# Two-layer graph attention on one core: float8 masks, an OR check of the kept masks, a reordered layer change and a last run closed in two halves

## The chip, the cores and the metric

The kernel runs on one core of one Trainium2 chip. The metric is the device time of one execution in microseconds, as the median of several runs. TensorE is called PE in the rows, VectorE DVE, ScalarE ACT, GpSimd POOL, SyncE SP.

## The reference

There are N = 4096 nodes with 128 features, an adjacency matrix adj of N x N int32 (0 or 1, some 0.2% ones, symmetric, ones on the diagonal), and two attention layers. Each is followed by a residual sum and a layer norm.

```python
# layer 0: H = 4 heads of D = 32
Wh = (h @ W).reshape(N, H, D)
e = s_src[:, None, :] + s_dst[None, :, :]          # per head, s = Wh . a
e = jnp.where(e >= 0, e, 0.2 * e)
e = jnp.where(adj[:, :, None] > 0, e, NEG_INF)
attention = jax.nn.softmax(e, axis=1)
h0 = jax.nn.elu(jnp.einsum('ijh,jhd->ihd', attention, Wh).reshape(N, H * D))
x = _layernorm(x + h0)
# layer 1: one head of 128
x_tan = _logmap0(x)
e = jax.nn.leaky_relu(x_tan @ a[:D] + (x_tan @ a[D:]).T, 0.2)
attention = jax.nn.softmax(jnp.where(adj > 0, e, NEG_INF), axis=1)
x = _layernorm(x + _proj(_expmap0(attention @ x_tan)))
```

## The kernel before

The attention is never formed. exp(leaky(s_i + d_j)) is a product of a factor of i and one of j on either side of the sign of s_i + d_j. So the kernel makes two 0/1 masks from the adjacency, the neighbours above and those below, and TensorE multiplies both with weighted features, split into three bf16 parts. The masks are float8, four to an int32.

**Masks.** GpSimd's queue loads the adjacency with a cast from int32 to one byte (adj_tiles). TensorE transposes the bytes in pairs, seen as bf16, and ScalarE copies them from the bank to masks, scaled so that a 1 becomes 0xC0 and a 0 becomes 0x80 (L451, L471). SyncE stores each of the four column blocks of masks (masks_kept, 4 MB each) for the second layer.

**First layer.** Four column blocks (NC) of 32 units each: ScalarE or VectorE makes the signs, VectorE the masks, TensorE the 64 matmuls (L613). take_head takes a head out of the banks, close_piece closes a block of rows (ELU, norm, the two dots for the second layer) in five pieces.

**Second layer.** 32 row tiles in NR = 8 runs of RT = 4 tiles. A run has 256 matmuls, two banks per tile, so all eight banks belong to one run. Its stationary operands are the masks, its moving ones the weighed features, in four groups (NG = 4) of 8 tiles. A group is made by weigh_group (VectorE, two sides), round_part1 (ScalarE cast), take_high1 (VectorE difference), round_part1 again and take_middle1. In runs 0 and 1 TensorE goes group by group (L972), from run 2 on tile by tile (L985). Groups 0 to 2 need nothing of the first layer's last block; group 3 needs all of close_piece, roots, logs and gains for it.

For a run e, SyncE loads its kept masks (load_masks, 2 MB) and scores (load_s1) when run e - 2 is done, ScalarE makes signs for half of the columns (signs, L695), VectorE compares the rest and splits the masks (split_group, L710 to L722). The banks are emptied by evacuate_run (L730), tile by tile, and finish_run closes the run: it asks ScalarE for a square root, a tanh and a square root (Closing.dve and Closing.act, L339). The order on VectorE after the first runs is: evacuate_run(e), finish_run(e), split_group(e + 2). TensorE begins tile t of run e + 1 when pair t of run e is out of the banks (pair_taken).

**Checks.** The masks hold only if adj has nothing but 0 and 1. 128 loads of 512 KB each bring all of adj once more, unchanged, to five buffers; ScalarE takes the square of 2a - 1 with a sum (check_part, L750), in batches after signs in runs 0 to 6. raise_flag (VectorE, after finish_run of run 6) waits for them all, joins them with the ranges of scores, and sends a flag that a general version would be chosen by; it then ends in nothing for these inputs.

All waits are written out as semaphores; each engine goes through its instructions in the order in which the code lists them.

Of the kernel before, what the change touches and what calls it, by code (L numbers as in the profile page):

```python
# [19 lines left out]
BOTH_SIGNS = float(0x8080)  # L20

# [40 lines left out]
def two_layer_gat(nc, x, adj, W, a0, a1, out):  # L62
# [8 lines left out]
    adj_flat = adj.rearrange("(p k) n -> p (k n)", p=P)  # L71
# [53 lines left out]
    CHECKS = 128  # L125
    CHECK = N * N // P // CHECKS
# [9 lines left out]
    with ctx:  # L136
# [19 lines left out]
        minus_one = sb("minus_one", [P, 1], F32, fast)  # L156
# [3 lines left out]
        checks = sb("checks", [P, CHECKS], F32, fast)  # L160
# [8 lines left out]
        adj_tiles = sb("adj_tiles", [P, AHEAD, N], U8, fast)  # L169
# [41 lines left out]
        def of_ring(*shape):  # L211
# [8 lines left out]
        late_sides = [of_ring(GT, K1).rearrange("p (t k) -> p t k", k=K1) for _ in range(2)]  # L220
# [11 lines left out]
            mean_var=of_ring(RT, 2).rearrange("p (t k) -> p t k", k=2))  # L232
        free = (NG - 1) * GT * W1
# [3 lines left out]
        check_out = [s_rows[:, 1, :].bitcast(FP8)[:, n * CHECK:(n + 1) * CHECK] for n in range(4)]  # L237
# [6 lines left out]
        def j_tile1(half, j):  # L244
# [28 lines left out]
        minus_ready, check_done, odd_ready, odd_in, flag_ready = sems(  # L273
            "minus_ready", "check_done", "odd_ready", "odd_in", "flag_ready")
# [5 lines left out]
        class Closing:  # L280


            def __init__(self, name, work, result, small, stats, mean_var, inv_std):
                self.work, self.result, self.small, self.stats, self.mean_var = work, result, small, stats, mean_var
                self.inv_std = inv_std
                self.asked, self.given, self.ready = sems(f"{name}_asked", f"{name}_given", f"{name}_ready")
                self.stored = sems(f"{name}_stored0", f"{name}_stored1")

            def dve(self, step, v, e):
                dve, y = step.engine, e % 2  # L290
                raw2, raw, scratch, norm, gain, big, root = (self.small[:, k, :] for k in range(7))
                work, result = self.work, self.result[:, y, :, :]
# [3 lines left out]
                dve.wait_ge(self.given, e * 3 + 1)  # L296
# [5 lines left out]
                inv = self.inv_std[:, e * RT:(e + 1) * RT]  # L302
                last = dve.tensor_tensor(result, feat[:, e * RT:(e + 1) * RT, :], over(inv, RT, F), ALU.mult)
                result_at = step.post(last)
                dve.wait_ge(self.given, e * 3 + 2)
# [10 lines left out]
                step(dve.tensor_tensor(work, v, over(gain, RT, F), ALU.mult))  # L316
                step.need(result_at)
                step(dve.tensor_tensor(result, result, work, ALU.add))
                for t in range(RT):
                    last = dve.bn_stats(self.stats[:, t, 0:6], result[:, t, :])  # L320
                step(last)
                for t in range(RT):
                    last = dve.bn_aggr(self.mean_var[:, t, :], self.stats[:, t, 0:6])
                step(last)
                dve.tensor_scalar(raw2, self.mean_var[:, :, 1], LN_EPS, None, ALU.add).then_inc(self.asked, 1)
                dve.wait_ge(self.given, e * 3 + 3)
                newton_root(step, root, raw2, scratch)
                step(dve.reciprocal(root, root))
                for t in range(RT):
                    last = dve.tensor_scalar(result[:, t, :], result[:, t, :], self.mean_var[:, t, 0:1], root[:, t:t + 1],  # L330
# [3 lines left out]
            def act(self, act, e):  # L334
                raw2, raw, scratch, norm, gain, big, root = (self.small[:, k, :] for k in range(7))
                for n, (to, frm, func) in enumerate(((raw, norm, ACT.Sqrt), (gain, scratch, ACT.Tanh),
                                                     (root, raw2, ACT.Sqrt))):
                    act.wait_ge(self.asked, e * 3 + (n + 1))
                    act.activation(to, frm, func).then_inc(self.given, 1)  # L339

            def store(self, sp, e):
                sp.wait_ge(self.ready, e + 1)
                sp.dma_start(out_rows[:, e * (RT // 2):(e + 1) * (RT // 2), :], paired(self.result[:, e % 2, :, :]))\
                    .then_inc(self.stored[e % 2], 16)

            def all_stored(self, sp):
                for y in range(2):
                    sp.wait_ge(self.stored[y], 16 * (NR // 2))
# [97 lines left out]
        def take_quarter(act, k, some=range(CT // 2)):  # L446
            for m in some:
# [5 lines left out]
                               ACT.Copy, bias=BOTH_SIGNS, scale=float(TWO)).then_inc(turned_out, 1)  # L453
# [13 lines left out]
        def take_group(act, c, q):  # L467
# [5 lines left out]
                           ACT.Copy, bias=BOTH_SIGNS, scale=float(TWO)).then_inc(turned_out, 1)  # L473
# [175 lines left out]

        def weigh_group(dve, g):  # L650
            sides = early_sides if g == 0 else late_sides
            js = slice(g * GT, (g + 1) * GT)
            for b in range(2):
                if g > 1:
                    dve.wait_ge(moving1_ready, 2 * g)
# [7 lines left out]
        def take_high1(dve, g):  # L663
            sides = early_sides if g == 0 else late_sides
            for b in range(2):
                dve.wait_ge(cast1_given, 4 * g + b + 1)
                dve.tensor_tensor(sides[b], sides[b], moving_part(g, b, 0), ALU.subtract).then_inc(cast1_asked, 1)

        def take_middle1(dve, g):
            sides = early_sides if g == 0 else late_sides  # L670
            for b in range(2):
                dve.wait_ge(cast1_given, 4 * g + 2 + b + 1)
# [3 lines left out]
        def round_part1(act, g, q):  # L676
            sides = early_sides if g == 0 else late_sides
            for b in range(2):
                act.wait_ge(cast1_asked, 4 * g + 2 * q + b + 1)
# [45 lines left out]
        def evacuate_run(dve, e):  # L725
            for t in range(RT):
# [723 lines left out]
```

## Time and profile before

| | before |
|---|---|
| median of 3 runs | 979.15 us (977.76 to 983.52) |
| the profiled execution's own time | 978.17 us |
| its span | 976.3 us |
| TensorE busy | 854.6 us (88%) |
| VectorE busy | 771.7 us (79%) |
| ScalarE busy | 759.4 us (78%) |
| first layer's matmuls end | about 558.4 us |
| last matmul ends | about 937.6 us |

A row of a timeline gives the start in us from the span's start, the duration, engine, line, operation, what is written and read, how many instructions were merged, and in brackets how long the engine idled before and what ended that. The page's groups give busy us and mean ns.

### The profile page before, as it was taken

What the parts mean: (1) busy time and instruction counts of PE and PEld (TensorE: products, weight loads), DVE (VectorE), ACT (ScalarE), POOL (GpSimd) and SP (SyncE); (2) the same over time, 40 slices, a digit from 0 to 9 for tenths busy, and PEclk for the clock granted to TensorE, in tenths of its full rate; (3) what the DMA queues carried; (4) which work ended last, traced back from release to release, by engine and by line L of the source; (5) the groups of instructions that cost most, each with busy time, mean ns of one, the idle gap of its engine ahead of it and who ended that gap; (6) DMA issues with size and microseconds to landing.
All of it is one profiled execution on the core that took longest, in us unless ns stands there. A gap on an engine that the chain in (4) does not pass through costs nothing.

```text
span 976.3 us, 24788 instructions
## 1 busy us (share of the span) xinstructions
PE 854.6 (88%) x10868; PEld 698.6 (72%) x10868; DVE 771.7 (79%) x1415; ACT 759.4 (78%) x933; POOL 94.9 (10%) x177
## 2 busy tenths in 40 slices
PE   8468999989999899999999992999999999899940
PEld 6468999989999899999998951555555555455520
DVE  3857898899988999889977897986859594949316
ACT  3868988888999879999889865367877686868751
POOL 2200000000000000000000100003131222212210
PEclk9879999999999999999999997899999999999975
DMA  8988278704568045040300040209494949576750
GB/s 143 172 83 203 64 71 95 222 24 49 66 75 228 24 39 73 25 196 23 110 3 24 19 177 1 98 12 361 170 388 152 402 152 368 190 308 220 279 211 12
DMA packets 55731, 135.01 MB, mean 138 GB/s; under 512 B 7746, under 2 KB 32708, under 8 KB 54980
## 3 DMA queue, kind: packets, MB, share of 16 engines
q0 software_dynamic: 26240, 83.90, 36.8%
q1 hardware_dynamic: 29380, 49.50, 13.9%
q8 instruction: 86, 1.41, 0.6%
q14 instruction: 25, 0.20, 0.1%
HBM read 162.60 MB, written 21.12 MB: 188 GB/s over the span
## 4 chain that ended last, share of the span: by engine, by line
PE 42%; DVE 26%; DMA 13%; ACT 11%; issue 7%; SPq 0%; DVEq 0%; ACTq 0%
PE bank L613 32%; DMA ring<-in_adj_dram 5%; PE bank L985 4%; ACT masks L695 4%; DMA moving<-in_adj_dram 4%; DVE ring L561 4%; DMA s_rows<-score_rows 3%; DVE ring L580 3%; ACT ring L548 2%; PE bank L464 2%; ACT s_rows L750 2%; ACT masks L451 2%; DVE ring L590 1%; PE bank L972 1%; DVE ring L584 1%
## 5 line engine op out<-in xcount | busy, mean ns | idle before, releaser
L613 PE MATMUL bank<-moving,ring 128*128 128x99 bf16 (+1 forms) x6400 | 461.8, 220 | 10.7 <-DVE ring L590 7.6
L613 PEld LDWEIGHTS bank<-moving,ring 128*128 128x128 fp8e4 x6400 | 390.9, 98 | 15.2 <-DVE ring L590 8.6
L548 ACT ACTIVATE ring<-s_rows,scores 128x1024 fp8e4<-128x1024 f32 x356 | 377.5, 1142 | 15.6 <-PE bank L613 14.2
L613 PE MATMUL bank<-moving,masks 128*128 128x99 bf16 x1792 | 243.3, 210 | 26.5 <-DVE ring L580 15.6
L613 PEld LDWEIGHTS bank<-moving,masks 128*128 128x128 fp8e4 x1792 | 176.7, 99 | 28.3 <-DVE ring L580 16.5
L985 PE MATMUL bank<-moving,masks 128*128 128x387 bf16 x1152 | 195.6, 328 | 0.0
L985 PEld LDWEIGHTS bank<-moving,masks 128*128 128x128 fp8e4 x1152 | 112.7, 98 | 79.1
L580 DVE SCALAR_TENSOR_TENSOR ring<-ring,masks 128x1024 int32<-128x1024 int32 x89 | 108.3, 1217 | 4.7 <-ACT ring L548 4.6
L590 DVE TENSOR_TENSOR ring<-masks,ring 128x1024 int32<-128x1024 int32 x72 | 88.2, 1225 | 26.4 <-PE bank L613 24.6
L750 ACT ACTIVATE s_rows<-moving,minus_one 128x1024 fp8e4<-128x1024 int32 x76 | 86.9, 1144 | 26.9 <-DMA moving<-in_adj_dram 26.3
L561 DVE TENSOR_SCALAR ring<-s_rows,neg_d 128x1024 uint8<-128x1024 f32 x156 | 106.9, 750 | 0.0
L695 ACT ACTIVATE masks<-s_rows,adj_tiles 128x512 fp8e4<-128x512 f32 x144 | 89.3, 709 | 1.1 <-DMA s_rows<-score_rows 0.9
L972 PE MATMUL bank<-moving,masks 128*128 128x387 bf16 x384 | 66.7, 335 | 20.6 <-DVE masks L722 20.6
L985 PE MATMUL bank<-adj_tiles,masks 128*128 128x387 bf16 x384 | 69.3, 333 | 11.9 <-DVE ring L730 11.9
L972 PEld LDWEIGHTS bank<-moving,masks 128*128 128x128 fp8e4 x384 | 38.0, 100 | 49.1 <-DVE masks L722 21.8
L750 ACT ACTIVATE s_rows<-ring,minus_one 128x1024 fp8e4<-128x1024 int32 x52 | 59.4, 1143 | 12.5 <-DMA ring<-in_adj_dram 12.2
L985 PEld LDWEIGHTS bank<-adj_tiles,masks 128*128 128x128 fp8e4 x384 | 37.6, 99 | 40.6 <-DVE ring L730 13.9
L471 ACT ACTIVATE masks<-bank 128x1024 uint16<-128x1024 uint16 x48 | 48.5, 1016 | 19.6 <-PE bank L464 18.6
L896 POOL DMA_DIRECT2D ring<-in_adj_dram x52 | 27.7, 533 | 357.2 <-PEq L621 180.8
L50 DVE TENSOR_SCALAR ring<-ring 128x4 f32<-128x4 f32 x16 | 2.7, 170 | 70.1 <-ACT ring L339 70.1
L896 POOL DMA_DIRECT2D moving<-in_adj_dram x76 | 40.8, 538 | 134.1 <-ACT s_rows L750 130.8
L584 DVE TENSOR_TENSOR ring<-ring,masks 128x1024 int32<-128x1024 int32 x39 | 47.5, 1218 | 0.0
(183 smaller groups left out, 750.6 us busy)
## 6 DMA issues: line engine op xcount, KB each, us to landing
moving<-in_adj_dram POOLq DMA_DIRECT2D x76, 512.0 KB, 6.6
ring<-in_adj_dram POOLq DMA_DIRECT2D x52, 512.0 KB, 6.3
masks_kept<-masks SPq DMA_DIRECT2D x4, 4096.0 KB, 18.4
masks<-masks_kept SPq DMA_DIRECT2D x8, 2048.0 KB, 23.7
adj_tiles<-in_adj_dram POOLq DMA_DIRECT2D x24, 512.0 KB, 8.4
s_rows<-score_rows SPq DMA_DIRECT2D x14, 512.0 KB, 5.7
adj_tiles<-in_adj_dram POOLq DMA_DIRECT2D x16, 256.0 KB, 15.1
feat<-in_x_dram SPq DMA_DIRECT2D x4, 512.0 KB, 5.7
```

The costliest lines, as they stand in the source:

```text
L471: act.activation(dst[:, j:j + GQ, t * P:(t + 1) * P], turn_bank[q % 4][:, :].bitcast(U16).rearrange("p (j i) -> p j i", i=P), ACT.Copy, bi ...
L548: last = act.activation(j_tile(below, k), s_rows[:, h % 2, :], ACT.Sign, bias=scores[:, g * JU + k, h:h + 1], saturate=False)
L561: last = dve.tensor_scalar(j_tile(below, k), s_rows[:, h % 2, :], neg_d[:, h, j:j + 1], float(TWO), ALU.is_lt, ALU.mult)
L580: dve.scalar_tensor_tensor(out=below, in0=below, scalar=1, in1=m, op0=ALU.logical_shift_right, op1=ALU.bitwise_and).then_inc(done, 1)
L584: dve.tensor_tensor(below, below, m, ALU.bitwise_and).then_inc(done, 1)
L590: dve.tensor_tensor(above_slot(c, u).bitcast(I32), m, below, ALU.bitwise_xor).then_inc(unit_ready, 1)
L613: last = pe.matmul(bank[b][:, at + lo:at + hi], mask, moving[:, j, h, lo:hi], start=first, stop=(j == T - 1), skip_group_check=True)
L695: last = act.activation(j_tile1(sides_of_run[y][1], j), s_rows1[:, y, :], ACT.Sign, bias=d1[:, j:j + 1], saturate=False)
L750: act.activation(check_out[k % 4], check_in[k % CB], ACT.Square, bias=minus_one[:, 0:1], scale=2.0, accum_out=checks[:, k:k + 1], saturate ...
L896: pool.dma_start(check_in[k % CB], adj_flat[:, k * CHECK:(k + 1) * CHECK]).then_inc(check_loaded[k % CB], 16)
L972: last = pe.matmul(bank[2 * t + side][:, 0:PARTS * K1], j_tile1(sides_of_run[e][side], j)[:, t * P:(t + 1) * P], moving1(g)[:, j % GT, sid ...
L985: last = pe.matmul(bank[2 * t + side][:, 0:PARTS * K1], j_tile1(sides_of_run[e % 2][side], j)[:, t * P:(t + 1) * P], moving1(j // GT)[:, j ...
```

## The change

1. The adjacency is cast to float8 instead of uint8 on its load. A 1 is then 0x38, and ScalarE's copies scale by 8/7 instead of 64 (0x38 x 8/7 = 0x40). Any value but 0 and 1 leaves other bits.
2. The check reads the kept masks (16 MB) and not the adjacency (64 MB): 32 loads of 512 KB, to two buffers instead of five, and 32 ORs on VectorE into one tile (seen), instead of 128 squares on ScalarE. raise_flag folds the tile to 64 words, takes the six low bits of each byte and their maximum.
3. The second layer's groups 1 to 3 have two pairs of buffers for the weighed sides. Groups 1 and 2 are weighed one behind the other, pieces of close_piece come in between, and ScalarE's order changes too.
4. The last run is emptied, closed and stored in two halves of two tiles; evacuate_run, finish_run and Closing get bounds lo and hi.

```diff
-    CHECKS = 128
-    CHECK = N * N // P // CHECKS
+    CHECKS = 32
+    CHECK = N * N // P // 4 // CHECKS
...
-        adj_tiles = sb("adj_tiles", [P, AHEAD, N], U8, fast)
+        adj_tiles = sb("adj_tiles", [P, AHEAD, N], FP8, fast)
...
-        late_sides = [of_ring(GT, K1).rearrange("p (t k) -> p t k", k=K1) for _ in range(2)]
+        late_sides = [[of_ring(GT, K1).rearrange("p (t k) -> p t k", k=K1) for _ in range(2)] for _ in range(2)]
...
-        check_in = [of_ring(CHECK).bitcast(I32) for _ in range(2)] + \
-            [moving_flat[:, free + n * 2 * CHECK:free + (n + 1) * 2 * CHECK].bitcast(I32) for n in range(3)]
+        seen, *check_in = [moving_flat[:, free + n * 2 * CHECK:free + (n + 1) * 2 * CHECK].bitcast(I32) for n in range(3)]
         CB = len(check_in)
...
-                               ACT.Copy, bias=BOTH_SIGNS, scale=float(TWO)).then_inc(turned_out, 1)
+                               ACT.Copy, bias=BOTH_SIGNS, scale=ONE_TO_TWO).then_inc(turned_out, 1)
...
-        def check_part(act, k):
-
-            act.wait_ge(check_loaded[k % CB], 16 * (k // CB + 1))
-            if k >= 4:
-                act.wait_ge(check_done, k - 3)
-            act.activation(check_out[k % 4], check_in[k % CB], ACT.Square, bias=minus_one[:, 0:1], scale=2.0,
-                           accum_out=checks[:, k:k + 1], saturate=False).then_inc(check_done, 1)
+        def check_part(dve, k):
+
+            dve.wait_ge(check_loaded[k % CB], 16 * (k // CB + 1))
+            dve.wait_ge(check_done, k + 1)
+            dve.tensor_tensor(seen, seen, check_in[k % CB], ALU.bitwise_or).then_inc(check_done, 1)
+
+        def begin_checks(dve):
+            dve.memset(seen, 0)
+            dve.memset(low_bits.bitcast(U8), 0x3F).then_inc(check_done, 1)
...
+            n = CHECK
+            while n > CHECK // 16:
+                n //= 2
+                step(dve.tensor_tensor(seen[:, 0:n], seen[:, 0:n], seen[:, n:2 * n], ALU.bitwise_or))
+            step(dve.tensor_tensor(seen[:, 0:n], seen[:, 0:n], low_bits, ALU.bitwise_and))
...
                 for k in range(CHECKS):
                     if k >= CB:
-                        pool.wait_ge(check_done, k - CB + 1)
-                    pool.dma_start(check_in[k % CB], adj_flat[:, k * CHECK:(k + 1) * CHECK]).then_inc(check_loaded[k % CB], 16)
+                        pool.wait_ge(check_done, k - CB + 2)
+                    if k == 0:
+                        pool.wait_ge(kept, 16 * NC)
+                    pool.dma_start(check_in[k % CB], kept_flat[k // (CHECKS // NC), :, (k % (CHECKS // NC)) * CHECK:
+                                                               (k % (CHECKS // NC) + 1) * CHECK]).then_inc(check_loaded[k % CB], 16)
...
@@ ScalarE, layer change @@
                 act.wait_ge(moving1_ready, 2)
+                elu_exp(act, NC - 1)
+                round_part1(act, 1, 0)
+                round_part1(act, 2, 0)
+                round_part1(act, 1, 1)
                 signs(act, 0, 1)
-                round_part1(act, 1, 0)
-                round_part1(act, 1, 1)
-                elu_exp(act, NC - 1)
+                round_part1(act, 2, 1)
                 signs(act, 0, 2)
-                round_part1(act, 2, 0)
-                round_part1(act, 2, 1)
...
@@ ScalarE, the runs @@
-                for e in range(NR):
-                    fast_closing.act(act, e)
+                for e in range(NR - 1):
+                    fast_closing.act(act)
                     if e + 2 < NR:
                         for g in range(NG):
                             signs(act, e + 2, g)
-                    while done < min(CHECKS, CHECKS * (e + 1) // (NR - 1)):
-                        check_part(act, done)
-                        done += 1
+                fast_closing.act(act, 0, RT // 2)
+                fast_closing.act(act, RT // 2, RT)
...
@@ VectorE, layer change @@
                 weigh_group(dve, 1)
+                weigh_group(dve, 2)
                 take_high1(dve, 1)
+                close_piece(NC - 1, 0)
                 take_middle1(dve, 1)
                 split_group(dve, 0, 1)
-                close_piece(NC - 1, 0)
-                weigh_group(dve, 2)
                 take_high1(dve, 2)
+                close_piece(NC - 1, 1)
                 take_middle1(dve, 2)
                 split_group(dve, 0, 2)
-                for n in range(1, 5):
+                for n in range(2, 5):
                     close_piece(NC - 1, n)
...
@@ VectorE, the runs @@
-                for e in range(NR):
+                done = 0
+                for e in range(NR - 1):
                     evacuate_run(dve, e)
...
                     if e + 2 < NR:
                         for g in range(NG):
                             split_group(dve, e + 2, g)
+                    if e == 0:
+                        begin_checks(dve)
+                    while done < CHECKS * max(e - 1, 0) // (NR - 3) and done < CHECKS:
+                        check_part(dve, done)
+                        done += 1
                     if e == NR - 2:
                         raise_flag(step)
+                for lo in (0, RT // 2):
+                    evacuate_run(dve, NR - 1, lo, lo + RT // 2)
+                    finish_run(step, NR - 1, lo, lo + RT // 2)
```

The change moves instructions at three places. The first is the layer change on ScalarE. Before, from the first set of signs of run 0 (L695) to the first casts of the second layer (L680) and ELU's exp (L646):

```order
L695 ACTIVATE masks<-s_rows,adj_tiles 128x512 x16
L680 ACTIVATE moving<-ring 128x8x129 x4
L646 ACTIVATE second_part<-first_part 128x1024
L695 ACTIVATE masks<-s_rows,adj_tiles 128x512 x8
L680 ACTIVATE moving<-ring 128x8x129 x4
```

Of the change, where these lines are L700, L685 and L648:

```order
L700 ACTIVATE masks<-s_rows,adj_tiles 128x512 x8
L648 ACTIVATE second_part<-first_part 128x1024
L685 ACTIVATE moving<-ring 128x8x129 x6
L700 ACTIVATE masks<-s_rows,adj_tiles 128x512 x8
L685 ACTIVATE moving<-ring 128x8x129 x2
L700 ACTIVATE masks<-s_rows,adj_tiles 128x512 x8
```

Of the sixteen signs, eight now stand behind the exp and six casts. The same place on VectorE, of the change, from the weighing of groups 1 and 2 (L661) over the differences (L672, L678), the ELU sums (L396, L398) and the norm's first piece (L403) to the splits (L720, L727):

```order
L672 TENSOR_TENSOR ring<-ring,moving 128x1032 x2
L396 SCALAR_TENSOR_TENSOR second_part<-second_part,feat 128x1024
L398 SCALAR_TENSOR_TENSOR second_part<-first_part,second_part 128x1024
L678 TENSOR_TENSOR moving<-ring,moving 128x8x129 x2
L720 SCALAR_TENSOR_TENSOR masks<-masks 128x1024
L727 TENSOR_TENSOR masks<-masks 128x1024
L672 TENSOR_TENSOR ring<-ring,moving 128x1032 x2
L403 BN_STATS stats<-second_part 128x6 x8
L678 TENSOR_TENSOR moving<-ring,moving 128x8x129 x2
```

Pieces of the closing now stand between the two differences of a group; before they stood behind the splits. The second place is VectorE between two runs: of the change, the end of the splits for run 4, the first batch of ORs (L756, the buffers are parts of moving), and run 3's sums out of the banks (L735):

```order
L715 TENSOR_SCALAR masks<-s_rows,adj_tiles 128x512 x4
L720 SCALAR_TENSOR_TENSOR masks<-masks 128x512
L725 TENSOR_TENSOR masks<-masks 128x512
L727 TENSOR_TENSOR masks<-masks 128x1024
L756 TENSOR_TENSOR moving<-moving 128x1024 x6
L735 TENSOR_REDUCE ring<-bank 128x129 x8
```

The six ORs are new there; before, the sums followed the splits. The third is VectorE after the closing of run 6, where raise_flag follows the last batch and the last run's sums come in two halves:

```order
L756 TENSOR_TENSOR moving<-moving 128x1024 x7
L798 TENSOR_TENSOR moving<-moving 128x512
L798 TENSOR_TENSOR moving<-moving 128x256
L798 TENSOR_TENSOR moving<-moving 128x128
L798 TENSOR_TENSOR moving<-moving 128x64
L799 TENSOR_TENSOR moving<-moving,ring 128x64
L801 TENSOR_REDUCE odd<-scores 128x1
```

The seven ORs and five folding steps are new ahead of the flag's own instructions.

## Rows read from the trace of the kernel before

**Rows 1.** The page: the span.
```profile
span 976.3 us, 24788 instructions
```
**Rows 2.** Timeline, TensorE: group 3, starts of runs 2 to 4, last stretch.
```profile
612.13 12.92 PE L972 MATMUL bank<-moving,masks 128*128 128x387 bf16 x64 [19.10 <-DVE masks L722]
...
667.50 2.83 PE L985 MATMUL bank<-adj_tiles,masks 128*128 128x387 bf16 x16
...
712.04 2.84 PE L985 MATMUL bank<-adj_tiles,masks 128*128 128x387 bf16 x16 [1.76 <-DVE ring L730]
...
757.05 2.84 PE L985 MATMUL bank<-adj_tiles,masks 128*128 128x387 bf16 x16 [2.23 <-DVE ring L730]
...
929.47 8.15 PE L985 MATMUL bank<-moving,masks 128*128 128x387 bf16 x48
```
**Rows 3.** Timeline, VectorE, three starts of L730; then the page's group of the wait.
```profile
665.93 3.82 DVE L730 TENSOR_REDUCE ring<-bank 128x129 f32<-128x387 f32 x8
...
710.96 3.82 DVE L730 TENSOR_REDUCE ring<-bank 128x129 f32<-128x387 f32 x8
...
730.39 0.17 DVE L50 TENSOR_SCALAR ring<-ring 128x4 f32<-128x4 f32 x1 [11.02 <-ACT ring L339]
...
755.97 3.82 DVE L730 TENSOR_REDUCE ring<-bank 128x129 f32<-128x387 f32 x8
...
L50 DVE TENSOR_SCALAR ring<-ring 128x4 f32<-128x4 f32 x16 | 2.7, 170 | 70.1 <-ACT ring L339 70.1
```
**Rows 4.** Timeline, VectorE, from the last wait to the end.
```profile
944.78 0.42 DVE L785 TENSOR_REDUCE odd<-scores 128x1 f32<-128x256 f32 x1 [24.79 <-ACT s_rows L750]
...
950.69 3.83 DVE L730 TENSOR_REDUCE ring<-bank 128x129 f32<-128x387 f32 x8
954.55 1.23 DVE L739 TENSOR_TENSOR ring<-ring,adj_tiles 128x1032 f32<-128x1032 f32 x1
...
963.29 0.69 DVE L316 TENSOR_TENSOR ring<-ring 128x512 f32<-128x512 f32 x1
...
964.74 0.87 DVE L320 BATCH_NORM_STATS2 ring<-ring 128x6 f32<-128x128 f32 x4
...
967.73 1.12 DVE L330 TENSOR_SCALAR ring<-ring 128x128 f32<-128x128 f32 x4
```
**Rows 5.** The page: a VectorE operation on two operands of 1024 int32.
```profile
L590 DVE TENSOR_TENSOR ring<-masks,ring 128x1024 int32<-128x1024 int32 x72 | 88.2, 1225 | 26.4 <-PE bank L613 24.6
```
**Rows 6.** DMA: issues at 658.61 and 659.74, all 128, a chain step, stores.
```profile
ring<-in_adj_dram POOLq DMA_DIRECT2D x1, 512.0 KB, 3.9
...
ring<-in_adj_dram POOLq DMA_DIRECT2D x1, 512.0 KB, 4.5
...
DMA to landing us min/median/max: 3.8/6.6/9.7
...
660.59 0.28 issue
...
out_dram<-ring SPq DMA_DIRECT2D x8, 256.0 KB, 2.2
```
**Rows 7.** Busy by stretch (us, PE, PEld, DVE, ACT, POOL, PEclk, DMA, GB/s); timeline, layer change.
```profile
560.00:580.00 20.00, 19.63 (x119) 11.35 (x118) 19.90 (x23) 15.69 (x18) 1.41 (x3) 1.00 0.63 236
...
560.55 1.22 DVE L656 TENSOR_TENSOR ring<-feat,adj_tiles 128x1024 f32<-128x1024 f32 x1
...
547.53 9.92 ACT L695 ACTIVATE masks<-s_rows,adj_tiles 128x512 fp8e4<-128x512 f32 x16
561.89 4.65 ACT L680 ACTIVATE moving<-ring 128x1032 bf16<-128x1032 f32 x4 [4.44 <-DVE ring L657]
...
567.38 5.00 ACT L695 ACTIVATE masks<-s_rows,adj_tiles 128x512 fp8e4<-128x512 f32 x8
```
**Rows 8.** DMA issues with a cast; busy by stretch, the first 50 us.
```profile
adj_tiles<-in_adj_dram POOLq DMA_DIRECT2D x24, 512.0 KB, 8.4
...
0.00:50.00 50.00, 31.54 (x245) 27.64 (x246) 29.80 (x64) 30.13 (x38) 12.70 (x25) 0.90 0.99 156
```

More of the change, by code:

```diff
@@ L287, in __init__, with dve @@
                 self.stored = sems(f"{name}_stored0", f"{name}_stored1")
[L289 to L292, printed above, removed]
+                self.turns, self.answers, self.stores = 0, 0, [0, 0]
+            def dve(self, step, v, e, lo=0, hi=RT):
+                dve, y, tiles = step.engine, e % 2, hi - lo
+                raw2, raw, scratch, norm, gain, big, root = (self.small[:, k, lo:hi] for k in range(7))
+                work, result = self.work[:, lo:hi, :], self.result[:, y, lo:hi, :]
+                before = self.turns
+                self.turns += 3
                 step(dve.tensor_tensor(work, v, v, ALU.mult))
@@ L315, in dve @@
                 step(dve.tensor_tensor(gain, gain, scratch, ALU.mult))
-                step(dve.tensor_tensor(work, v, over(gain, RT, F), ALU.mult))
+                step(dve.tensor_tensor(work, v, over(gain, tiles, F), ALU.mult))
                 step.need(result_at)
                 step(dve.tensor_tensor(result, result, work, ALU.add))
-                for t in range(RT):
-                    last = dve.bn_stats(self.stats[:, t, 0:6], result[:, t, :])
+                for t in range(tiles):
+                    last = dve.bn_stats(self.stats[:, lo + t, 0:6], result[:, t, :])
@@ L321, in dve @@
                 step(last)
-                for t in range(RT):
-                    last = dve.bn_aggr(self.mean_var[:, t, :], self.stats[:, t, 0:6])
+                for t in range(tiles):
+                    last = dve.bn_aggr(self.mean_var[:, lo + t, :], self.stats[:, lo + t, 0:6])
                 step(last)
-                dve.tensor_scalar(raw2, self.mean_var[:, :, 1], LN_EPS, None, ALU.add).then_inc(self.asked, 1)
-                dve.wait_ge(self.given, e * 3 + 3)
+                dve.tensor_scalar(raw2, self.mean_var[:, lo:hi, 1], LN_EPS, None, ALU.add).then_inc(self.asked, 1)
@@ L327, in dve @@
+                dve.wait_ge(self.given, before + 3)
                 newton_root(step, root, raw2, scratch)
                 step(dve.reciprocal(root, root))
-                for t in range(RT):
-                    last = dve.tensor_scalar(result[:, t, :], result[:, t, :], self.mean_var[:, t, 0:1], root[:, t:t + 1],
+                for t in range(tiles):
+                    last = dve.tensor_scalar(result[:, t, :], result[:, t, :], self.mean_var[:, lo + t, 0:1], root[:, t:t + 1],
                                              ALU.subtract, ALU.mult)
@@ L332, in dve, with act @@
                 last.then_inc(self.ready, 1)
[L334 to L338, printed above, removed]
+            def act(self, act, lo=0, hi=RT):
+                raw2, raw, scratch, norm, gain, big, root = (self.small[:, k, lo:hi] for k in range(7))
+                for to, frm, func in ((raw, norm, ACT.Sqrt), (gain, scratch, ACT.Tanh), (root, raw2, ACT.Sqrt)):
+                    self.answers += 1
+                    act.wait_ge(self.asked, self.answers)
```

86 lines of the change are left out of this document (43 added, 43 removed).

## The prediction

> **What bounds the kernel now.** I read the page first, then TensorE's timeline through the second layer, then VectorE's, then the DMA issues. The span is 976.3 us [rows 1], of which TensorE is busy for the greatest part. In the second layer its runs of 256 matmuls follow each other: run 2 starts at 667.50, run 3 at 712.04 after 1.76 us of waiting, run 4 at 757.05 after 2.23. A run thus takes 712.04 - 1.76 - 667.50 = 42.8 us [rows 2]. The waits, 11.9 us in five places, are all for VectorE's sums out of the banks (L730). The last matmul ends near 937.6.
>
> VectorE's loop explains them [rows 3]. From one L730 to the next (710.96 to 755.97) it takes 45.0 us, of which it idles 11.0 at L50: it has asked ScalarE for a square root (L339), and ScalarE first finishes its batch of adjacency checks (L750). Over six runs these idles are 10.96, 11.02, 10.76, 13.11, 11.88 and 8.31, together 66.0 of the page's 70.1 us. Without the idle (some 0.27 is left of it where ScalarE is free: the group's ten others share 4.1 us) the loop is 45.0 - 10.75 = 34.3 us: 3.9 of L730, 14.3 of closing, 16.1 of splitting masks for the run after next. So VectorE has 42.8 - 34.3 = 8.5 us of slack per run, or about 10 when its first sums of a run lie under TensorE's work.
>
> The tail [rows 4]: VectorE waits 24.8 us, until 944.78, for the last check, raises the flag (5.9 us), and only at 950.69 takes the last run out of the banks, though TensorE was done 13 us before. The closing ends at 968.85, the store and the rest of the program take 7.4 more.
>
> **Part 1, the checks.** 128 ScalarE instructions with 128 loads of the adjacency go; 32 ORs on VectorE with 32 loads of the kept masks come. ScalarE's 146 us of checks and 48 MB of the traffic go, and with them the 66.0 us of idle (1.6 stays) and the 24.8. What comes: an OR of 1024 int32 is priced by L590, the same shape and kind, 1.23 us, 1.25 with its semaphore [rows 5]. They stand in batches of 6, 6, 7, 6, 7 after the splits of runs 2 to 6, ahead of the next L730. Six would be 7.5 us and would fit the slack, if their data were there.
>
> But the five landing buffers become two. A buffer's next load is issued only when its OR is done, and VectorE then waits out the whole latency with L730 queued behind. The rows give that latency [rows 6]: a 512 KB load issued alone lands 3.9 us after its issue (658.61), the one issued 1.1 us behind it 4.5; the least of all 128 is 3.8; the step from the check to the issue is 0.28. The median of 6.6 belongs to five in flight. So a pair of ORs costs 1.22 + 0.28 + 3.9 + 0.05 = 5.45 us and not 2.5. A batch of six, whose first two loads are there: OR 3 starts at 5.45, OR 5 at 10.9, OR 6 ends near 13.7; with the second load of a pair 0.3 late, 14.0. A batch of seven: OR 7 starts at 16.35 and ends at 17.6. Sum of five batches: 14.0 x 3 + 17.6 x 2 = 77.2 us. Twelve latencies lie in it, so one microsecond more or less in the latency moves it by 12.
>
> The page "DMA: Bandwidth & Descriptors" of the Trainium skill (Anatomy of one DMA) gives 2.0 us plus bytes over 436 GB/s, that is 3.2 us for 512 KB as an estimate. The lone loads took 3.9 here, so the trace does not agree; by the page's figure the forecast would be 8 us lower. The measured 3.9 stands in the sum.
>
> **Part 2, the layer change.** VectorE's work from 560.55 to group 3's masks is the same and has no idle to be removed: it is busy for 19.90 of the 20 us from 560 to 580 [rows 7]. So two buffer pairs can't shorten it; the 19.1 us wait of TensorE before 612.13 [rows 2] ends when this chain ends. What moves is ScalarE. Before, it made the signs of groups 0 and 1 (9.92 us from 547.53) while it was free. Now the second 8 signs stand behind ELU's exp, which waits for the last head, and behind six casts. Followed through: weigh 1 and 2 to 565.5, first difference to 567.9, ELU sum to 570.2, second difference to 572.6. ScalarE: exp to 561.8, casts (1.16 each) to 569.05, signs (5.0) to 574.05. VectorE waits 1.4. Its next difference asks at 577.65; ScalarE casts to 580.1, makes signs to 585.1; VectorE is there at 582.9 and waits 2.2. Sum 3.6 us later, all on the chain that ends at 612.13. The bounds: 0, if ScalarE's work were covered after all, and 5, one whole set of signs on the path.
>
> **Part 3, memsets and the flag.** Two memsets stand ahead of run 1's L730, which began at 665.93 [rows 3], 1.6 before TensorE was through. No row shows one; bounded by 0.2 (a small instruction) and 1.2 (a pass over 1024 words); I take 1.3 for both, as a pass. TensorE then starts run 2 1.08 behind that L730 (757.05 - 755.97), at 665.93 + 3.6 + 1.3 + 1.08 = 671.9. The flag gets five halving steps, 512 to 64 words, by the rows of 0.69 for 512 and 0.17 for the smallest about 2.1: 8.0 us.
>
> **Part 4, the last run in halves.** The closing of a half: the long instructions halve (L739 saves 0.54, seven of 0.69 save 0.27 each, L320, L323 and L330 half of 2.4; [rows 4]), the some twenty short ones stay. Sum 3.6. So 14.3 - 3.6 = 10.7, with 1.9 of L730 12.6 to 12.7. Two are 25.4 against 18.2 for the whole. That pays only if the first half is done under TensorE's last tiles.
>
> **Part 5, the cast to float8.** The loads of the adjacency (8.4 us median) [rows 8] move as many bytes, the transposes and copies have the same shapes: 0. No row shows a float8 cast; the bound is 0 below, and above I leave some 10 us for a slower one, since in the first 50 us the DMA engines are busy for 0.99 of the time [rows 8].
>
> **The sum.** TensorE's run 2: 671.9 to 714.7; its last tile is out of the bank at 715.9. VectorE: + 30.4 + 14.0 = 760.3. TensorE's run 3 ended at 757.5, so it waits, and VectorE is the bound from here. + 34.3 + 14.0 = 808.6 (run 4 ended 804.2); + 34.3 + 17.6 = 860.5; + 34.3 + 14.0 = 908.8; run 6: + 3.9 + 14.3 + 17.6 + 8.0 = 952.6. TensorE's run 7 goes from 909.9 to 952.7, so the first half finds VectorE busy with checks and flag and isn't hidden; + 25.4 = 978.0. Mask transfers (2 MB, started at a run's end) now meet the last loads of the batches of runs 3 and 4: 0 to 4 us, I take 1. End 979 against 968.85: + 10. The profiled execution's own 978.2 becomes 988.2; the median of the three runs is 1.0 above it, so 989.2.
>
> **The rivals.**
> *The checks hide (faster).* If the ORs waited for nothing, batches of 7.5 and 8.75 fit the slack; TensorE sets the pace: run 7 ends at 714.7 + 5 x 42.8 = 928.7, VectorE's two halves at some 943: - 25, 954. The gain of over 1% begins where the end is 19 us below my sum, at a latency of 3.9 - 19/12 = 2.3 us. No 512 KB load shows under 3.8; only the 256 KB stores land in 2.2 [rows 6]. Chance 0.10, with a nearly as good result by other slack I misread.
> *The latency is shorter, or the layer change costs nothing (970 to 985).* A store of 256 KB lands in 2.2 us; the second of two loads lands 1.1 + 4.5 - 3.9 = 1.7 us behind the first, so 256 KB more cost some 0.85: 3.05 us [rows 6]. With that and 0 in part 2: 989 - 10 - 3.6 = 975. For it: the kept masks of neighbouring partitions lie 32 KB apart, the adjacency's 512 KB. Against it: no load of 512 KB landed in under 3.8. Chance 0.27.
> *Loads meet the masks, or the float8 cast is slower (998 and over).* With 4.5 in place of 3.9 us, + 7; a cast, + 10. The first pair of rows speaks for 4.5 only where two are in flight. Chance 0.10.
> *My forecast,* 985 to 998: 0.53.
>
> **How the numbers follow.** 1% is about what a measurement of this kernel can tell from no change: 969.4 and 988.9. My case lies across the upper one: of its 0.53 some 0.33 is above. Slower 0.33 + 0.10 = 0.43; within 1% 0.20 + 0.25 = 0.45; faster 0.10 + 0.02 = 0.12. The range 968 to 999 leaves out the first rival and the end of the last.
>
> **What would show it.** In the trace of after: ScalarE answers L50 within 0.3 us; ORs in pairs with VectorE idle some 3 us before every other one, released by DMA; TensorE waits of 3 to 9 us at each of the runs 4 to 7, for the sums; group 3 near 615.7; first half closed only after 952. The forecast is wrong if the ORs stand 1.25 us apart, if TensorE's runs stay 42.8 apart, or if the first 100 us lengthen.

## The result

The change makes the kernel slower. The median of four runs is 992.84 us (990.38 to 993.78), against 980.96 us before; the ratio is 1.0123 with a 95% interval of 1.0087 to 1.0159. The forecast was 989.2 us in a range of 968 to 999. Slower by over 1%, which the ratio came out as, had a chance of 0.43, and within 1% had 0.45; the interval's lower end lies within 1%.

Below is the page of the changed kernel: the span, the groups of the ORs (L756) and of the later runs' matmuls (L1004), and the loads with their median time to landing.

```profile
span 992.0 us, 24425 instructions
PE 861.7 (87%) x10868; PEld 701.6 (71%) x10868; DVE 819.1 (83%) x1488; ACT 608.9 (61%) x682; POOL 43.2 (4%) x80
...
L1004 PE MATMUL bank<-adj_tiles,masks 128*128 128x387 bf16 x384 | 74.4, 350 | 22.6 <-DVE ring L735 22.6
...
L756 DVE TENSOR_TENSOR moving<-moving 128x1024 int32<-128x1024 int32 x32 | 39.2, 1224 | 43.1 <-DMA moving<-masks_kept 42.6
...
moving<-masks_kept POOLq DMA_DIRECT2D x32, 512.0 KB, 4.0
```

ScalarE's work fell by 150 us and VectorE's waits for its square root are down to 0.3 us each. But VectorE now idles 42.6 us for the ORs' loads, with its sums out of the banks (L735, once L730) queued behind, and TensorE waits 22.6 us for those, where it waited 11.9.

VectorE's timeline from its last sums of run 2 to the first of run 3 shows one burst:

```profile
716.77 1.03 DVE L735 TENSOR_REDUCE ring<-bank 128x129 f32<-128x387 f32 x2 [7.35 <-PE bank L1004]
...
748.25 2.55 DVE L756 TENSOR_TENSOR moving<-moving 128x1024 int32<-128x1024 int32 x2
753.62 1.23 DVE L756 TENSOR_TENSOR moving<-moving 128x1024 int32<-128x1024 int32 x1 [2.81 <-DMA moving<-masks_kept]
756.09 1.22 DVE L756 TENSOR_TENSOR moving<-moving 128x1024 int32<-128x1024 int32 x1 [1.25 <-DMA moving<-masks_kept]
758.94 1.23 DVE L756 TENSOR_TENSOR moving<-moving 128x1024 int32<-128x1024 int32 x1 [1.62 <-DMA moving<-masks_kept]
761.39 1.23 DVE L756 TENSOR_TENSOR moving<-moving 128x1024 int32<-128x1024 int32 x1 [1.23 <-DMA moving<-masks_kept]
762.54 3.82 DVE L735 TENSOR_REDUCE ring<-bank 128x129 f32<-128x387 f32 x8
```

The first two ORs find their data; each later one waits. The burst takes 762.54 - 748.25 = 14.3 us, of which 7.5 are ORs. TensorE's starts of runs 3 to 7 answer [rows 2]:

```profile
716.58 2.82 PE L1004 MATMUL bank<-adj_tiles,masks 128*128 128x387 bf16 x16
...
763.62 5.35 PE L1004 MATMUL bank<-adj_tiles,masks 128*128 128x387 bf16 x16 [4.26 <-DVE ring L735]
...
812.28 2.84 PE L1004 MATMUL bank<-adj_tiles,masks 128*128 128x387 bf16 x16 [3.08 <-DVE ring L735]
...
866.73 5.28 PE L1004 MATMUL bank<-adj_tiles,masks 128*128 128x387 bf16 x16 [11.67 <-DVE ring L735]
...
915.51 4.49 PE L1004 MATMUL bank<-adj_tiles,masks 128*128 128x387 bf16 x16 [3.55 <-DVE ring L735]
```

From start to start, a run took 44.5 to 47.1 us before (runs 5 to 7 started at 801.79, 848.89 and 894.84); here runs 3 to 6 take 47.0, 48.7, 54.5 and 48.8. The 54.5 belongs to run 5, whose end waits for a burst of seven ORs. The end answers [rows 4]: flag, first half's sums, second half's sums, last instruction.

```profile
953.14 0.42 DVE L801 TENSOR_REDUCE odd<-scores 128x1 f32<-128x256 f32 x1
...
959.22 1.96 DVE L735 TENSOR_REDUCE ring<-bank 128x129 f32<-128x387 f32 x4
...
971.93 1.96 DVE L735 TENSOR_REDUCE ring<-bank 128x129 f32<-128x387 f32 x4
...
984.12 0.60 DVE L331 TENSOR_SCALAR ring<-ring 128x128 f32<-128x128 f32 x2
```

TensorE's last matmul ends at 959.95, so the first half was begun with three quarters of a microsecond of cover.

**A measure without the first layer's scatter.** In the twelve profiles TensorE begins the second layer between 557.4 and 563.0 us, with no pattern by change. So beside the times I compare the stretch G from there (group 0's first matmul) to the last closing instruction. Before: 968.85 - 559.06 = 409.8. The change: 984.72 - 562.57 = 422.2. The difference of 12.4 fits the 11.9 of the medians.

### The profile page after: what moved, and what is told of

Its sections match the earlier page's. It is cut to its first block, busy times and chain, and to the rows that moved or that the text cites. A ratio compares the mean times of both kernels' runs of the same rounds, so it can differ in the third digit from the quotient of the medians.

```text
span 992.0 us, 24425 instructions
## 1 busy us (share of the span) xinstructions
PE 861.7 (87%) x10868; PEld 701.6 (71%) x10868; DVE 819.1 (83%) x1488; ACT 608.9 (61%) x682; POOL 43.2 (4%) x80
## 4 chain that ended last, share of the span: by engine, by line
PE 46%; DVE 36%; ACT 7%; DMA 6%; issue 5%; SPq 0%; POOL 0%; DVEq 0%; ACTq 0%; POOLq 0%
PE bank L615 32%; PE bank L991 6%; DMA moving<-masks_kept 5%; PE bank L1004 4%; DVE ring L563 4%; DVE ring L582 3%; DVE masks L715 3%; ACT ring L550 2%; PE bank L466 2%; DVE moving L756 2%; DVE ring L735 2%; DVE masks L727 2%; ACT masks L453 1%; ACT masks L700 1%; DVE ring L592 1%
## 5 line engine op out<-in xcount | busy, mean ns | idle before, releaser
L1004 PE MATMUL bank<-moving,masks 128*128 128x387 bf16 x1152 | 196.0, 328 | 0.0
L340 ACT ACTIVATE ring<-ring 128x4 f32<-128x4 f32 (+1 forms) x27 | 5.5, 205 | 269.0 <-DVE ring L296 234.5
L1004 PEld LDWEIGHTS bank<-moving,masks 128*128 128x128 fp8e4 x1152 | 113.0, 98 | 79.7 <-issue 0.9
L1004 PE MATMUL bank<-adj_tiles,masks 128*128 128x387 bf16 x384 | 74.4, 350 | 22.6 <-DVE ring L735 22.6
L700 ACT ACTIVATE masks<-s_rows,adj_tiles 128x512 fp8e4<-128x512 f32 x144 | 89.3, 711 | 0.1
L1004 PEld LDWEIGHTS bank<-adj_tiles,masks 128*128 128x128 fp8e4 x384 | 39.3, 103 | 53.9 <-DVE ring L735 24.1
L756 DVE TENSOR_TENSOR moving<-moving 128x1024 int32<-128x1024 int32 x32 | 39.2, 1224 | 43.1 <-DMA moving<-masks_kept 42.6
L715 DVE TENSOR_SCALAR masks<-s_rows,adj_tiles 128x512 uint8<-128x512 f32 x112 | 46.7, 482 | 0.0
L631 DVE TENSOR_REDUCE evac<-bank 128x132 f32<-128x396 f32 x64 | 32.9, 562 | 15.1 <-PE bank L615 14.6
L914 POOL DMA_DIRECT2D moving<-masks_kept x32 | 17.0, 531 | 550.8 <-DVE moving L756 366.1
## 6 DMA issues: line engine op xcount, KB each, us to landing
adj_tiles<-in_adj_dram POOLq DMA_DIRECT2D x16, 256.0 KB, 15.4
```

The lines of the kernel that those rows point to most:

```text
L700: last = act.activation(j_tile1(sides_of_run[y][1], j), s_rows1[:, y, :], ACT.Sign, bias=d1[:, j:j + 1], saturate=False)
L715: last = dve.tensor_scalar(j_tile1(below.bitcast(U8), j), s_rows1[:, y, :], neg_d1[:, j:j + 1], float(TWO), ALU.is_lt, ALU.mult)
L756: dve.tensor_tensor(seen, seen, check_in[k % CB], ALU.bitwise_or).then_inc(check_done, 1)
L1004: last = pe.matmul(bank[2 * t + side][:, 0:PARTS * K1], j_tile1(sides_of_run[e % 2][side], j)[:, t * P:(t + 1) * P], moving1(j // GT)[:, j ...
```

## The experiments

Times are medians; ratios are to the kernel before, measured on the same chip. The chips differ: e1 to e4 ran on one (before: 980.55), e5 to e8 on a second (982.23), e9 and e10 on a third (980.51), and the change with the result (980.96). So between experiments of different chips G and the ratios compare better than the times. G is from one profile of each kernel.

| run | us | ratio (95%) | G, us |
|---|---|---|---|
| before | 980.55 | 1 | 409.8 |
| the change | 992.84 | 1.0123 (1.0087 to 1.0159) | 422.2 |
| e1_cast_alone | 979.92 | 0.9990 (0.9974 to 1.0006) | 410.4 |
| e2_layer_as_before | 988.62 | 1.0085 (1.0061 to 1.0110) | 418.6 |
| e4_last_whole | 983.67 | 1.0038 (1.0016 to 1.0060) | 413.9 |
| e9_one_buffer | 1070.56 | 1.0908 (1.0848 to 1.0968) | 501.9 |
| e3_spread | 950.43 | 0.9699 (0.9672 to 0.9722) | 379.8 |
| e8_no_checks | 948.60 | 0.9668 (0.9645 to 0.9690) | 378.8 |
| e6_spread_whole | 951.74 | 0.9695 (0.9671 to 0.9719) | 382.1 |
| e7_five_buffers | 952.09 | 0.9678 (0.9651 to 0.9704) | 380.5 |
| e5_spread_layer | 945.41 | 0.9637 (0.9615 to 0.9659) | 376.6 |
| e10_norm_first | 942.89 | 0.9608 (0.9574 to 0.9641) | 373.0 |

**The cast.** Before with two edits:

```diff
-        adj_tiles = sb("adj_tiles", [P, AHEAD, N], U8, fast)
+        adj_tiles = sb("adj_tiles", [P, AHEAD, N], FP8, fast)
-    ACT.Copy, bias=BOTH_SIGNS, scale=float(TWO))
+    ACT.Copy, bias=BOTH_SIGNS, scale=8.0 / 7.0)
```

The scale stands at both copies (L451, L471).

> The kernel before with the float8 cast of the adjacency and the scale of 8/7 alone. In the profile of the change the first layer ends 3.5 us later than before (TensorE's group 0 at 562.57 against 559.06), which no step of the prediction has. Theory: the cast costs nothing, the 3.5 us are scatter between executions; the time is that of before, 979 to 982 us. Rival: the float8 cast lengthens the loads or the copies; the time is 3 to 4 us above before, 983 to 986, and group 0 starts near 562.5 in this profile as well.

Measured 979.92, ratio 0.999. Its loads land after 8.4 us like those of before [rows 8]. The cast costs nothing that can be measured. Group 0 started at 561.66 in this profile, nearer the rival's 562.5 than 559.06, so that sign alone doesn't decide. What does are the median and the other profiles: e3, which has the cast too, started group 0 at 557.42, earlier than before. The first layer's end is scatter.

**The layer change alone.** The change with the lines of before at the layer change on both engines; the second pair of buffers stays. The cut shows the beginning of ScalarE's part.

```diff
                 act.wait_ge(moving1_ready, 2)
-                elu_exp(act, NC - 1)
-                round_part1(act, 1, 0)
-                round_part1(act, 2, 0)
-                round_part1(act, 1, 1)
                 signs(act, 0, 1)
...
```

> The change with the layer change put back to the old order (one behind the other, signs of group 1 early), all else as in the change. Theory: eight signs on VectorE's path cost 3.2 to 3.6 us and all of it reaches the end, since VectorE is the bound from run 3 on: 989 to 990 us against 992.8, and TensorE's wait before group 3 grows from 15 back to 19 us while group 3 starts earlier. Rival: the order costs nothing, since VectorE's work is the same; 992 to 993. Second rival: the new order pays, 995 or more.

Measured 988.62, 4.2 below the change; G says 3.6. From group 0 to group 3 it takes 613.66 - 560.60 = 53.06 us, against 618.89 - 562.57 = 56.32. VectorE's timeline of the change has both waits that were foreseen:

```profile
577.30 1.23 DVE L720 SCALAR_TENSOR_TENSOR masks<-masks 128x1024 int32<-128x1024 int32 x1 [1.35 <-ACT masks L700]
...
588.10 1.22 DVE L720 SCALAR_TENSOR_TENSOR masks<-masks 128x1024 int32<-128x1024 int32 x1 [2.20 <-ACT masks L700]
```

In the profile of before the same two instructions have no wait:

```profile
567.72 1.22 DVE L715 SCALAR_TENSOR_TENSOR masks<-masks 128x1024 int32<-128x1024 int32 x1
...
579.68 1.22 DVE L715 SCALAR_TENSOR_TENSOR masks<-masks 128x1024 int32<-128x1024 int32 x1
```

**The bursts taken apart.** The same ORs, loads and buffers, in other places.

```diff
                     evacuate_run(dve, e)
+                    if e > 0: check_part(dve, done); done += 1
...
                     finish_run(step, e)
+                    if e > 0: check_part(dve, done); done += 1
                     if e + 2 < NR:
                         for g in range(NG):
                             split_group(dve, e + 2, g)
+                            if e > 0: check_part(dve, done); done += 1
-                    while done < CHECKS * max(e - 1, 0) // (NR - 3) and done < CHECKS:
-                        check_part(dve, done)
-                        done += 1
```

> The change with the same 32 ORs and the same two landing buffers, but the ORs taken apart: in runs 1 to 5 one after the sums, one after the closing and one after each of the four split groups, in run 6 two. Theory (the latency of loads in a burst costs some 37 us of VectorE's path): the waits for loads vanish, VectorE's loop is 34.3 + 7.5 = 41.8 us, TensorE sets the pace with 42.7 a run and the halves of the last run pay: 949 to 953 us. Rival: the sheer work of 32 ORs on VectorE is too much; the time stays within 5 us of the change, 988 to 993. Between, 955 to 975, if the loads in mid-run collide with the mask transfers.

Measured 950.43: 42 us below the change. VectorE's timeline of this run has an OR every 5.2 us while it splits masks, none of the 32 with a wait for a load, and it is back at the banks before TensorE is done with them (1.59 us of waiting for it):

```profile
781.56 1.22 DVE L756 TENSOR_TENSOR moving<-moving 128x1024 int32<-128x1024 int32 x1
...
786.74 1.22 DVE L756 TENSOR_TENSOR moving<-moving 128x1024 int32<-128x1024 int32 x1
...
791.92 1.22 DVE L756 TENSOR_TENSOR moving<-moving 128x1024 int32<-128x1024 int32 x1
793.05 2.89 DVE L735 TENSOR_REDUCE ring<-bank 128x129 f32<-128x387 f32 x6
797.53 1.03 DVE L735 TENSOR_REDUCE ring<-bank 128x129 f32<-128x387 f32 x2 [1.59 <-PE bank L1004]
```

TensorE has no wait in runs 2 to 7 here. The ORs and the bytes are the same as in the change, so it was neither the ORs' work nor the amount of their traffic.

**The last run in one piece**, on the burst order and on the spread one:

```diff
-                for lo in (0, RT // 2):
-                    evacuate_run(dve, NR - 1, lo, lo + RT // 2)
-                    finish_run(step, NR - 1, lo, lo + RT // 2)
+                evacuate_run(dve, NR - 1)
+                finish_run(step, NR - 1)
```

> The change with the last run emptied, closed and stored in one piece. Theory: VectorE comes to the last run only when TensorE is nearly through it, so the first half hides nothing and two halves cost 25.4 us against 18.2: 7 us less, 985 to 986.5 us. Rival: the halves pay through the earlier start of the first store and of the first half, and the time is 995 to 1000 without them.

> e3_spread with the last run in one piece. Theory: the halves pay only where VectorE is back before TensorE's last tiles, and here it is; one piece leaves 1.2 + 14.3 us behind the last matmul and two halves 1.2 + 10.7, so one piece costs 3.6 us: 953.5 to 954.5 us. Rival: the halves cost some 7 to 9 us here as well, as they did in the burst order: 942 to 944.

On the burst order one piece is 9.2 us faster by the times and 8.3 by G; about 1.6 of this is that the burst of seven took 862.20 - 843.63 = 18.6 us in this profile and 20.2 in that of the change, which leaves 6.7, near the 7.2 expected. The time, 983.67, fell below the 985 to 986.5 expected in part for the same reason. On the spread order one piece is slower: from the last matmul's end to the last closing instruction it takes 942.00 - 926.62 = 15.4 us, with halves 937.22 - 925.33 = 11.9. The 3.5 us are those expected; the medians differ by 1.3 and G by 2.3, less, because TensorE's group 3 ran 1.1 us faster in the one-piece profile (12.18 against 13.33 us for its 64 matmuls; the mean granted clock was 0.88 and 0.80 of full speed there). The median of 951.74 lies below the 953.5 to 954.5 expected and is nearly as high as that of e3, so that halves gain here is read from the tail of the two profiles; the medians alone don't show it. The same edit thus loses 7 us or gains about 3, by whether VectorE is free when TensorE is half through the last run.

**Five buffers.** e2_layer_as_before with room for five:

```diff
-        late_sides = [[...] for _ in range(2)]
+        late_sides = [[...]] * 2
         seen, *check_in = [...]
+        check_in += [of_ring(CHECK).bitcast(I32) for _ in range(2)] + [s_rows[:, 1, :].bitcast(I32)]
```

> e2_layer_as_before (988.6 us) with five landing buffers instead of two: two of the room of the second buffer pair, one of scores of the first layer. The ORs stay in bursts of 6, 6, 7, 6, 7. Theory (it is the loads' latency behind two buffers, not the burst): all loads but the last of a burst are there, a burst takes 7.5 to 9 us, VectorE's loop fits TensorE's run, 947 to 951 us. Rival (the burst itself ahead of the sums is the cost): 984 to 989. With five loads in flight landing in 6.6 us as before the change, 3 to 5 us more.

With the second pair gone, weigh_group waits for its buffers as it did before the change. Measured 952.09 in place of 988.62, bursts and all; 947 to 951 were expected. With five buffers the loads land after 5.0 to 5.3 us (medians), and a burst still finds nearly all of them landed. The burst of run 2 now takes 754.08 - 746.30 = 7.8 us:

```profile
746.30 2.55 DVE L757 TENSOR_TENSOR moving<-moving 128x1024 int32<-128x1024 int32 x2
748.95 2.55 DVE L757 TENSOR_TENSOR moving<-moving,ring 128x1024 int32<-128x1024 int32 x2
751.61 1.23 DVE L757 TENSOR_TENSOR moving<-moving,s_rows 128x1024 int32<-128x1024 int32 x1
752.94 1.23 DVE L757 TENSOR_TENSOR moving<-moving 128x1024 int32<-128x1024 int32 x1
754.08 2.89 DVE L736 TENSOR_REDUCE ring<-bank 128x129 f32<-128x387 f32 x6
```

It ends 3.9 us of G above the spread kernel of the same layer order (e5): in run 6 the seven ORs in a row, the flag and the first half fill VectorE until 930.7, 2.8 us after TensorE's last matmul, so the second half starts late:

```profile
930.71 1.95 DVE L736 TENSOR_REDUCE ring<-bank 128x129 f32<-128x387 f32 x4
```

**One buffer.** `range(3)` became `range(2)` where the buffers are cut out.

> The change with one landing buffer instead of two, the ORs in the same bursts. Every OR but the first of a burst then waits out a whole latency, 1.22 + 0.28 + 4.0 + 0.05 = 5.55 us. Theory (VectorE's path holds each exposed latency in full): a burst of six takes 1.2 + 5 x 5.55 = 29.0 us and one of seven 34.5, in sum 156 us against the 82 of the change; VectorE is the bound throughout, so the time is 993 + 74 = 1065 to 1068 us. Rival (part of the latency is hidden under TensorE's runs): below 1050.

Measured 1070.56, above the 1065 to 1068 expected; G + 79.7 where 74 were. VectorE's timeline:

```profile
751.99 1.23 DVE L756 TENSOR_TENSOR moving<-moving 128x1024 int32<-128x1024 int32 x1 [4.25 <-DMA moving<-masks_kept]
757.27 1.23 DVE L756 TENSOR_TENSOR moving<-moving 128x1024 int32<-128x1024 int32 x1 [4.05 <-DMA moving<-masks_kept]
766.32 1.23 DVE L756 TENSOR_TENSOR moving<-moving 128x1024 int32<-128x1024 int32 x1 [7.82 <-DMA moving<-masks_kept]
771.59 1.22 DVE L756 TENSOR_TENSOR moving<-moving 128x1024 int32<-128x1024 int32 x1 [4.05 <-DMA moving<-masks_kept]
```

A piece with a lone load takes 5.3 us against 5.55 reckoned, except the one whose load (issued at 758.79) lies beside the 2 MB mask transfer (issued at 757.66) at the run's end: 7.8 us of waiting. The bursts of runs 3 and 4 have one such piece each, with 7.2 and 8.0 us; those of runs 5 and 6, where no masks are loaded any more, have none. The five bursts take 160.8 us in place of 156, so these three collisions outweigh what the shorter pieces save.

**No checks.** The ORs and loads of e3_spread left out.

> e3_spread with the 32 ORs and their 32 loads left out (the kept masks aren't looked at; memsets, folding and flag stay). Theory: spread out, the ORs lie wholly in VectorE's slack of 8.5 us a run and cost nothing: 949 to 951 us, as e3_spread. Rival: they still hold TensorE up by one or two us a run, 940 to 945.

Measured 948.60; ratio 0.9668 against 0.9699, with intervals that overlap, G 1.0 us lower. Spread out, the check of 16 MB costs 1 us by G and 3 by the ratios, which is hardly clear of noise; in bursts behind two buffers it cost 422.2 - 378.8 = 43. That 43 holds the cover that the last run's first half lost as well.

**Both orders mended, and one more.** e5 is e3_spread with the old layer change:

> e3_spread with the layer change in the old order as well. Over six profiles group 3 starts 56.3 us behind group 0 with the new order and 53.06 with the old. Theory: those 3.25 us reach the end here too, since TensorE sets the pace from group 3 on: 946.5 to 947.5 us against 950.4. Rival: with TensorE as the bound the delay is absorbed in VectorE's slack: 950 to 951.

Measured 945.41, G 3.2 lower. G fell by the 3.25 expected and no slack absorbs it; the time fell by 5, below the 946.5 to 947.5 expected, but on another chip. e10 goes on from there. The cut shows VectorE's part; ScalarE's order changes with it.

```diff
-                close_piece(NC - 1, 0)
-                weigh_group(dve, 2)
-                take_high1(dve, 2)
-                take_middle1(dve, 2)
-                split_group(dve, 0, 2)
-                for n in range(1, 5):
+                for n in range(5):
                     close_piece(NC - 1, n)
                 roots_ask(...)
+                weigh_group(dve, 2)
                 dve.wait_ge(roots_given, 2)
                 logs_ask(...)
+                take_high1(dve, 2)
                 dve.wait_ge(logs_given, 2)
                 gains(...)
                 late_weights(1)
+                take_middle1(dve, 2)
+                split_group(dve, 0, 2)
                 weigh_group(dve, 3)
```

> e5_spread_layer (945.4 us) with another order at the layer change: after group 1, VectorE goes through all five pieces of the last block's closing, and group 2's weighing and differences fill the waits for ScalarE's root, logarithm and casts; ScalarE makes the last signs while it waits. One buffer pair. Theory (group 3 hangs on VectorE's chain, which idled 1.7 us at the root and the logarithm and 4.6 us at group 3's cast): group 3's masks are ready some 6 us earlier, at 47 us behind group 0 instead of 53; TensorE's group 2 goes before them and the time is 940 to 942 us. Rival: the waits only move, group 2 now starts so late that TensorE waits the same in sum: 944 to 946.5.

Measured 942.89, the fastest of all, 3.9% below before; G is 3.6 below e5. That is just above the 940 to 942 expected. Group 3's masks are ready at 609.86, 48.8 us behind group 0 and not 47: 4.2 us earlier than in e5, where 6 were expected (in e5 they are ready at 611.88, with group 0 at 558.90). TensorE's timeline shows groups 2 and 3 in one stretch of 128 matmuls behind a single wait; the row of VectorE stands below:

```profile
600.35 23.55 PE L991 MATMUL bank<-moving,masks 128*128 128x387 bf16 x128 [17.26 <-DVE masks L727]
623.74 10.81 PE L991 MATMUL bank<-adj_tiles,masks 128*128 128x387 bf16 x64
```

```profile
608.63 1.23 DVE L727 TENSOR_TENSOR masks<-masks 128x1024 int32<-128x1024 int32 x1
```

This row is the last step of group 3's masks in e10; in e5 it started at 610.66. Run 1 starts 62.7 us behind group 0; in e5 it was 625.17 - 558.90 = 66.3, and before the change 624.89 - 559.06 = 65.8.

**What the four edits make together.** Of the 12.4 us of G by which the change is slower, 3.6 go with the layer change (e2) and 8.3 with the halves of the last run (e4). If the two add up, which no run tried, the ORs in their bursts cost about as much as the 128 squares that they replaced, and the gain that e3 shows was lost to the bursts behind two buffers.

## Why the prediction was right

The forecast's steps were right in kind. That the sum came so near is in part luck: two misses of opposite sign met in it.

*What bounds the kernel.* Right. The loop of 34.3 us and the slack were VectorE's: in the change, sums to burst is 796.81 - 762.54 = 34.3.

*Part 1.* The mechanism was right and the term too small: five bursts took 14.3, 14.4, 20.2, 14.5 and 18.6 us, 82.0 against 77.2 and 1 for collisions. The latency of a pair's first load was right (3.7 to 3.9). The second's, for which some 4.2 were taken, is 4.9 to 5.1 in a burst's first pair, where it is issued 1.3 us behind the first; issued 2.3 to 2.9 us behind it, in the second pair, it is 3.8 to 4.1 (4.8 once, beside a mask transfer). The seventh OR's load took 6.9 beside the mask transfer issued at 855.10. In run 6 it took 5.0 with no such transfer, and why is open. The chain of the change has a second load, a first one and the one beside the masks, in order of time:

```profile
751.10 4.97 DMA moving<-masks_kept
...
846.99 3.76 DMA moving<-masks_kept
...
857.59 6.90 DMA moving<-masks_kept
```

The estimate by the Trainium skill's fit ("DMA: Bandwidth & Descriptors", Anatomy of one DMA), 3.2 us for 512 KB, does not agree with the traces: the least of the 32 loads of the one-buffer run landed after 3.6 us, the median after 3.8.

*Part 2.* Right: 3.26 us against 3.6, by waits of 1.35 and 2.20 against 1.4 and 2.2.

*Part 3.* The memsets took 0.91 and 0.27, 1.2 against 1.3. But VectorE came to them 1.6 us sooner than reckoned: the first closing's wait for its square root fell from 1.6 to 0.3 us. So the memsets held nothing up: TensorE starts run 2 at 673.97 without a wait, where the forecast had it 0.8 us late (671.9 in place of 667.50 + 3.6). The flag took 8.1 against 8.0.

*Part 4.* Right: 984.72 - 959.22 = 25.5 us for two halves against 25.4, with nothing hidden.

*Part 5.* Right: 0, by e1.

*The sum.* The end of the closing, counted from group 0, was put at 979 - 559.1 = 419.9 and came at 422.2. What is missing are the five bursts (+ 3.8 beyond the 1 that was taken for collisions), less 1.6 by which VectorE came earlier to the first burst: 748.25 - 562.57 = 185.68 against 715.9 + 30.4 - 559.06 = 187.24. Of this 1.6 some 0.3 are part 2 and 0.8 the memsets; the rest wasn't traced. The median came 3.6 us above the 989.2, 2.3 of it by this; the forecast stood on a median before of 979.15, which a fourth run moved to 980.96.

*The signs.* TensorE's waits at runs 4 to 7 were 4.3, 3.1, 11.7 and 3.6 us, where 3 to 9 had been named, and VectorE idled 2.7 to 2.9 us before the third OR of a burst, as named, but also 1.1 to 2.4 us before each of the next three.

*The rivals.* That the checks hide was wrong for this order and right for the order of e3 and for five buffers, by 42 and 36 us. That the latency is shorter found no support: no load of the change landed in under 3.7 us, nor was the layer change free. That the loads meet the masks came true in part, in one burst of the change; the cast did not slow it.

## What to carry to other kernels

Work that is moved off a busy engine must be priced with its loads: of n operations behind b landing buffers in one burst the first b find their data, and each further group of b exposes about one latency, for which whatever is queued behind pays (43 us here with two buffers, another 80 with one). Laid one by one between other work of the same engine, the same operations with the same two buffers cost 1 to 3 us. More buffers do nearly the same (five: 36 us back). Closing a last stage in parts pays only if the closing engine is free while the other still works, so it should be judged after its cover has been measured, not before: here it cost some 7 us without cover and gained about 3 with it.

## What was not expected

ScalarE's table load before the first square root of the second layer ran behind the wait before the change and ahead of it after, where one wait (for the constant -1) had gone. The first row is of before, on ScalarE:

```profile
638.75 1.28 ACT L339 ACT_TABLE_LOAD   x1 [20.72 <-DVE ring L295]
```

The second is of the change:

```profile
624.80 1.28 ACT L340 ACT_TABLE_LOAD   x1
645.17 0.20 ACT L340 ACTIVATE ring<-ring 128x4 f32<-128x4 f32 x1 [19.09 <-DVE ring L296]
```

That took 1.3 us off VectorE's wait there. Whether the missing wait is the cause was not tried.

TensorE's clock also moved small sums. In the change the first 16 matmuls of run 4, after 4.26 us of idle, took 5.35 us at a mean granted clock of 0.50 of full speed, the lower of its two levels (1.2 GHz); those of run 5, after 3.08 us, took 2.84 at 1.00 (2.4 GHz). The length of the idle alone doesn't sort them: in e1 they took 4.49 us (0.61) after 2.52 us of idle, and 2.84 (1.00) after 2.59.
